# A neighbour-maximum kernel whose last late round stands behind its loop and makes no further one-hots

## The reference, cut to what matters

```
h = maximum(layernorm(x), 0)
for every node: the 25 first neighbours (lowest index j with adj[i, j] != 0)
agg = maximum over those neighbours of h[j]        # feature by feature
agg = maximum(agg, 0) where the node has 25 or fewer neighbours
out = x + relu(concat(h, agg) @ W + b)
```

## Time and profile before

| | us |
|---|---|
| three executions | 699.74, 697.43, 698.69 |
| their median | 698.69 |
| the profiled execution | 697.45 |
| its span in the profile | 695.7 |
| outside the span | 1.75 |

### The profile page before, as it was taken

How to read it: one execution, slowest core, us unless ns; L and a number is a source line. 1 busy time by engine, 2 the same in 40 slices (tenths; PEclk the granted TensorE clock), 3 DMA queues, 4 the chain that set the end, 5 groups by cost and what they waited for, 6 DMA issues and landing times.

```text
span 695.7 us, 10819 instructions
## 1 busy us (share of the span) xinstructions
PE 630.9 (91%) x3376; PEld 297.4 (43%) x3376; DVE 613.7 (88%) x813; ACT 472.3 (68%) x642; POOL 50.3 (7%) x41
## 2 busy tenths in 40 slices
PE   2479998999989999899999999899999999999976
PEld 2133443535445354443545344353535335353423
DVE  3368999899998999989998899989998899988997
ACT  2689478783777639775795947777497927959120
POOL 1300021000210002100030002100021000300000
PEclk9899999999999999999999999999999999999999
DMA  9520141510415103251303313151122411020100
GB/s 361 199 87 27 60 152 68 182 70 16 152 73 200 60 15 136 83 188 60 128 23 122 151 60 151 68 196 57 41 122 87 185 60 32 16 107 1 60 15 16
DMA packets 19127, 67.64 MB, mean 97 GB/s; under 512 B 4499, under 2 KB 7830, under 8 KB 16534
## 3 DMA queue, kind: packets, MB, share of 16 engines
q1 hardware_dynamic: 19094, 67.26, 25.7%
HBM read 42.08 MB, written 4.19 MB: 67 GB/s over the span
## 4 chain that ended last, share of the span: by engine, by line
PE 66%; DVE 16%; issue 10%; ACT 4%; DVEq 1%; DMA 1%; POOL 1%; ACTq 0%
PE picked L506 18%; PE picked L507 17%; PE ring L455 14%; DVE late_hot L684 4%; PE side L469 4%; PE ring L449 4%; DVE hot L659 4%; PE side L463 4%; DVE best L775 3%; DVE best L678 3%; PE final L534 2%; PE final L538 2%; PE final L491 1%; DMA adj_in<-in_adj_dram 1%; DVEq L771 1%
## 5 line engine op out<-in xcount | busy, mean ns | idle before, releaser
L678 DVE TENSOR_TENSOR best<-picked,best 128x1024 f32<-128x1024 f32 x224 | 270.5, 1218 | 38.2 <-PE picked L507 36.0
L506 PE MATMUL picked<-hot,h_hi 128*128 128x512 f16 x512 | 194.5, 380 | 15.0 <-DVE best L775 7.5
L507 PE MATMUL picked<-hot,h_lo 128*128 128x512 f16 x512 | 194.0, 379 | 0.0
L506 PE MATMUL picked<-late_hot,hi_skew 128*128 128x512 f16 x336 | 127.6, 380 | 13.1 <-DVE late_hot L684 8.2
L507 PE MATMUL picked<-late_hot,lo_skew 128*128 128x512 f16 x336 | 127.3, 379 | 0.0
L344 ACT ACTIVATE late_rank<-ring,late_bias 128x512 bf16<-128x512 f32 x128 | 81.4, 690 | 57.6 <-PE ring L455 57.6
L775 DVE TENSOR_TENSOR best<-picked,best 128x1024 f32<-128x1024 f32 x84 | 102.4, 1219 | 8.3 <-PE picked L507 8.2
L378 ACT COPY best<-picked 128x1024 f32<-128x1024 f32 x32 | 32.2, 1013 | 102.6 <-PE picked L507 102.6
L659 DVE TENSOR_SCALAR hot<-rank 128x4096 f16<-128x4096 bf16 x64 | 89.4, 1399 | 12.0 <-ACT rank L344 12.0
L349 ACT ACTIVATE past<-side,bias_cut 128x512 bf16<-128x512 f32 x128 | 88.3, 690 | 6.2 <-PE side L469 4.9
L344 ACT ACTIVATE rank<-ring,bias_big 128x512 bf16<-128x512 f32 x128 | 83.1, 692 | 5.2 <-PE ring L455 4.9
(11 more groups left out here) (76 smaller groups left out, 562.1 us busy)
## 6 DMA issues: line engine op xcount, KB each, us to landing
adj_in<-in_adj_dram SPq DMA_DIRECT2D x16, 2048.0 KB, 7.7
late_skew<-late SPq DMA_DIRECT2D x32, 192.0 KB, 2.3
x_in<-in_x_dram SPq DMA_DIRECT2D x8, 512.0 KB, 8.5
xres<-in_x_dram SPq DMA_DIRECT2D x16, 256.0 KB, 7.8
late_skew<-late SPq DMA_DIRECT2D x16, 256.0 KB, 2.4
late_skew<-late SPq DMA_DIRECT2D x32, 128.0 KB, 2.0
out_dram<-xres SPq DMA_DIRECT2D x16, 256.0 KB, 2.0
late_skew<-late SPq DMA_DIRECT2D x32, 64.0 KB, 1.9
```

The costliest lines, as they stand in the source:

```text
L506: nc.tensor.matmul(dst, hi[:, slot, k, :], onehot, start=start, stop=False)
L507: return nc.tensor.matmul(dst, lo[:, slot, k, :], onehot, start=False, stop=stop)
L678: nc.vector.tensor_tensor(best[:, half, s, :, :], picked[s][:, :, :], best[:, half, s, :, :], ALU.max).then_inc(picked_read, 1)
```

## The change

The last round of each group no longer stands in the loop. TensorE gets a function `late_round`, DVE a function `take_late`. Both loops run one round fewer than the count (the constant at L667 is lowered by 1), but at least one; behind each loop the last round is written out. There DVE takes the two maxima and makes no one-hots. A group whose count was 1 now runs two rounds; the second finds one-hots that mark nothing. The register `rounds_done` goes up by one more behind the loop, and the wait for the one-hots no longer adds the group's number, since there is now one call of `make_late_hot` per round and half.

```diff
--- before.py
+++ after.py
@@ -539,6 +539,18 @@
                                             start=False, stop=(q == Q - 1))
                 last.then_inc(final_written, 1)
 
+            def late_round(g, done, r, slot):
+
+                for s in range(2):
+                    pe.wait_ge(picked_read, (g + 1) * READ - 1 + s)
+                    pe.wait_ge(late_hot_made[s], done + r + 1)
+                    pe.wait_ge(late_read[s], done + r + 1)
+                    for j in range(2):
+                        for i in range(LINK):
+                            k = s * HALF + j * LINK + i
+                            last = pick(picked[s][:, j, :], hi_skew, lo_skew, k, late_hot[:, k, :], slot, i == 0, i == LINK - 1)
+                    last.then_inc(late_written[s], 1)
+
             rounds_done = pe.alloc_register("pe_rounds_done")
             pe.reg_mov(rounds_done, 0)
 
@@ -592,16 +604,11 @@
                 pe.wait_ge(rounds_known, g + 1)
                 n = pe.value_load(late_rounds[0:1, u % 2:u % 2 + 1], min_val=1, max_val=NEIGHBOURS)
                 with pe.Fori(0, n) as r:
-                    for s in range(2):
-                        pe.wait_ge(picked_read, (g + 1) * READ - 1 + s)
-                        pe.wait_ge(late_hot_made[s], done + (r + (g + 1)))
-                        pe.wait_ge(late_read[s], done + r + 1)
-                        for j in range(2):
-                            for i in range(LINK):
-                                k = s * HALF + j * LINK + i
-                                last = pick(picked[s][:, j, :], hi_skew, lo_skew, k, late_hot[:, k, :], slot, i == 0, i == LINK - 1)
-                        last.then_inc(late_written[s], 1)
+                    late_round(g, done, r, slot)
                 pe.reg_add(rounds_done, rounds_done, n)
+                done = pe.snap(rounds_done)
+                late_round(g, done, 0, slot)
+                pe.reg_add(rounds_done, rounds_done, 1)
 
                 if more:
                     done = pe.snap(rounds_done)
@@ -664,7 +671,7 @@
                 nc.vector.tensor_reduce(late_most[:, :], final[:, :], AX.X, ALU.max).then_inc(late_reduced, 1)
                 dve.wait_ge(late_reduced, (CHAINS + 1) * g + 1)
                 for c in range(CHAINS):
-                    nc.vector.tensor_scalar(late_other[:, c:c + 1], late_most[c * PART:c * PART + 1, :], LINK * P / 2, 1.0, ALU.add,
+                    nc.vector.tensor_scalar(late_other[:, c:c + 1], late_most[c * PART:c * PART + 1, :], LINK * P / 2 - 1, 1.0, ALU.add,
                                             ALU.max).then_inc(late_reduced, 1)
                 dve.wait_ge(late_reduced, (CHAINS + 1) * (g + 1))
                 nc.vector.tensor_reduce(late_rounds[0:1, s:s + 1], late_other[:, :], AX.X, ALU.max).then_inc(rounds_known, 1)
@@ -677,6 +684,12 @@
                 dve.wait_ge(picked_written, g * USES + use + 1)
                 nc.vector.tensor_tensor(best[:, half, s, :, :], picked[s][:, :, :], best[:, half, s, :, :],
                                         ALU.max).then_inc(picked_read, 1)
+
+            def take_late(s, i, done, r):
+
+                dve.wait_ge(late_written[i], done + r + 1)
+                nc.vector.tensor_tensor(best[:, s, i, :, :], picked[i][:, :, :], best[:, s, i, :, :],
+                                        ALU.max).then_inc(late_read[i], 1)
 
             def make_late_hot(i, which):
 
@@ -771,11 +784,13 @@
                 n = dve.value_load(late_rounds[0:1, s:s + 1], min_val=1, max_val=NEIGHBOURS)
                 with dve.Fori(0, n) as r:
                     for i in range(2):
-                        dve.wait_ge(late_written[i], done + r + 1)
-                        nc.vector.tensor_tensor(best[:, s, i, :, :], picked[i][:, :, :], best[:, s, i, :, :],
-                                                ALU.max).then_inc(late_read[i], 1)
+                        take_late(s, i, done, r)
                         make_late_hot(i, numbers[:, bass.ds(r + 2, 1)])
                 dve.reg_add(rounds_done, rounds_done, n)
+                done = dve.snap(rounds_done)
+                for i in range(2):
+                    take_late(s, i, done, 0)
+                dve.reg_add(rounds_done, rounds_done, 1)
                 done = dve.snap(rounds_done)
                 for i in range(2):
                     dve.wait_ge(late_read[i], done + 1)
```

## The result

The changed kernel takes 704.91 us (median of 6 executions, 703.62 to 707.86), the kernel before 698.56 us on the same chip (697.43 to 699.74). The ratio is 1.0089, 95% interval 1.0072 to 1.0106: slower by some 6.3 us. The profiled execution took 705.20 us with a span of 703.5 us, against 697.45 and 695.7 before.

The account below looks back on a forecast made before the run. TensorE was taken as busiest, the DVE close behind and the bound in the last two groups. Second round +3.47, one-hots -0.7 and -1.18, refetch +3.5 gave +5.1 us: 702.5, or 703.8 us as a median; range 700.2 to 705.6.

Parts of the forecast that it names:

- step 1: DVE's 16 last late rounds: 32 one-hots go, 19.8 us less work, counted as no time.
- step 2: One-hot 0 of the last round in 14 groups: removing it gains 0.05 us each, -0.7 us.
- step 3: Last two groups, where the DVE is the bound: 0.59 us gained in each, -1.18 us together.
- step 4: Second round for the group with one: costs 3.47 us, bounds 3.0 and 3.96.
- step 5: Register waits and sums outside the loop: cost nothing, at most 0.2 us or so per group.
- step 6: TensorE's longer program at the outer loop's two wraps: refetch of 1.75 us each, +3.5 us, bounds 0 and 2.4 each.
- One sign: DVE's idle time around use 5: expected to grow from 0.59 towards 1.2 us.
- The reason given for the refetch: TensorE's outer loop: about 150 more instructions bring one more packet in the first pass, so the loop's head is lost.
- A: Outer loop's wrap: TensorE keeps its loop's head, no refetch; +1.6 us, 700.3 us; chance 0.17.
- B: Late rounds: both one-hots on the path in every group; 691.6 us, or 695.1 with the refetch; chance 0.04.
- C: Heavier wrap: TensorE's sequencer no longer ahead, straight rounds 0.2 us each; +9.2 us, 707.9 us; chance 0.04.
- the likeliest case: Whole kernel, with the refetch as priced: 703.8 us, bounds 701.3 to 705.6; chance 0.75.

Follow-up runs that it names:

- experiment 10: Changed kernel with its last late round making two one-hots again, into a tile nobody reads: 706.27 us, ratio 1.0101.
- experiment 1: Changed kernel with TensorE doing every late round in its loop again, at least two; the DVE's part stays: 701.31 us, ratio 1.0049.
- experiment 8: Kernel before with the DVE's part of the change alone, one-round group staying at one round: 697.12 us, ratio 0.9968.
- experiment 2: Kernel before with the count of late rounds raised to at least two, nothing else: 703.37 us, ratio 1.0056.
- experiment 3: Kernel before with 16 empty instructions in TensorE's outer loop, in its fourth group: 701.49 us, ratio 1.0034.
- experiment 4: Kernel before with 16 empty TensorE instructions behind the outer loop, in the fourteenth group: 698.57 us, ratio 0.9992.
- experiment 5: Kernel before with 64 empty instructions in TensorE's outer loop, in its fourth group: 714.36 us, ratio 1.0212.
- experiment 7: Kernel before with 64 empty instructions at the very start of TensorE's program, loop body length unchanged: 703.6 us, ratio 1.0071.
- experiment 12: Changed kernel with the branch hint on TensorE's outer loop, measured again beside the unhinted changed kernel: 700.22 us, ratio 1.0014.
- experiment 6: Changed kernel with a prefetch hint for the branch back to the head of TensorE's outer loop: 700.28 us, ratio 1.0016.
- experiment 11: Changed kernel itself, unaltered, measured again beside its hinted form: 706.83 us, ratio 1.0100.

## Why the prediction was right

The forecast was 703.8 us, in a range of 700.2 to 705.6; measured 704.91. The sign, the cause and both large terms hold. That the sum comes so near is in part luck. In the profiles the last L538 comes 7.57 us later, where the steps say 5.1: the refetch is 0.85 more than I had, the start 1.38 and the last two groups 0.82 more, both with the clock fallen, and the rest 0.57 less. By its steps:

1. DVE work down by 19.8 us, no time: x86 and x86 as forecast. Busy time is 599.6 rather than 594, because the records overlap on both sides: the take at 163.49 ends at 164.72 and the next begins at 165.29, so a one-hot of 742 ns adds only 0.57 us of busy time. With that the step gives 14.7 us; measured are 14.1. It is no part of the sum.
2. One-hot 0 at 0.05 us a group: near in size (-1.20 us over 13 groups is 0.09 each), but by luck. About 0.05 lies behind the last late matmul, the rest is 0.03 a round inside the loop, and both stand in experiment 10 too, where the one-hots are made. The kernels that have this gain (the changed one in all its forms, experiments 1 and 8) share the shorter sum in TensorE's wait for the one-hots; the others (2 to 5 and 7) lack both. That this is the reason was not tested by itself.
3. The last two groups at 0.59 each: measured 0.46 and 0.51. The fold follows the last take by 1.33 us (166.53 to 167.85 above, and 686.13 to 687.46 in experiment 8) and not by 1.25. In group 15 the gain did come through whole, as chosen, and not only the 0.27 of the lower bound; in the changed kernel's profile the clock then fell to 0.59 in 682:686, which took it back. Where it stayed at 1.00 and the one-hots are gone (experiments 1, 8 and 12), the stretch to group 16 is 0.48 to 0.49 us shorter than before.
4. The second round, +3.47: measured +3.38 in the changed kernel and +3.48 in experiment 2.
5. Register waits at nothing: right in size. The small gaps ahead of late rounds sum to 0.42 us; their cause stays open.
6. The refetch, 1.75 each: the existence was right, in 6 of 6 wraps of the changed kernel and its version with the one-hots. The size was too small. In profiles the pieces are 2.10 to 2.73, over the chosen 1.75 and in three of six over the upper bound of 2.4; with the fall of the clock the two wraps are 6.43 (2.44, 1.70 and 2.29) in one profile, and 6.6 by medians, where I had 3.5. The branch record was 3.6 to 4.2 us where I had 3.1 to 3.6. The packet was not the error: it took 1.03 and 1.08 us, and I had 1.20. The time around it is longer, 2.6 and 2.7 us (3.2 and 3.3 in experiment 10), where ACT's rows gave me 1.9 to 2.2. The packet that follows (216.4 us) starts after the branch record has ended at 215.65 and is no part of the wait.

One sign was misplaced. The DVE's idle time at use 5 should have grown from 0.59 towards 1.2 us; it is 0.59 still. The DVE waits out what it gained one step earlier, for the projection's result: 0.62 us at 174.96 in the row above, where in the profile of before it is 0.16.

The reason given for the refetch was half right. One packet more is fetched in the first pass, while TensorE is still in the loop, as the prediction said. What I took it to mean, as the expectation of experiment 5 puts it, was that the body no longer fits with its head. Experiment 6 shows that it does fit, and experiment 7 that a body of the old length is refetched when it lies elsewhere. What matters is whether the place where TensorE fetches ahead lies inside the loop. The Trainium skill (Runtime: NRT & Kernel Launch, Instruction fetch mechanics) says that prefetch is purely sequential into a first-in first-out memory. The packets bear that out without a hint; with it the prefetch past the end of the loop is not made, which the page doesn't say. That this packet pushes the head out is my reading of experiments 6 and 7 and of the packets at all 28 wraps; no row shows directly what TensorE holds.

Of the rivals, A (no refetch, +1.6 us) is what the hinted kernel is: +1.4 us by the second batch's medians and +0.4 by the third's, ratios 1.0016 and 1.0014. B needed slack in picked1, and the 0.66 us of waiting shows there was none. C is partly there: the range's upper end of 705.6 is passed by the 706.83 of experiment 11, and for the reason of a heavier wrap, though not by a sequencer that had fallen behind, as C had it, but by the clock. The lower end of the likeliest case, 701.3, took 1.1 us for a refetch; no row gives that number, and step 6 has 0 as its bound.

Open stays why the packet ahead is fetched at one wrap and not at the other of the same execution, in experiments 1 and 3. The miss goes with that packet both times. What decides on it no run tested.

## What to carry to other kernels

Before writing out a loop's last pass, count what the outer loop gains in code on the busiest engine, and look in the packets of that engine's queue whether its loop fetches in its second pass; instructions ahead of the loop can bring that about too (experiment 7). If it does, try the branch hint first: here one argument gave back 6.6 of 7.1 us, side by side. And peel a loop only on the engine that gains: the DVE's half alone is 1.7 us faster than before, the change with TensorE's half is 6.3 us slower. An operation named by the chain of waits is worth only the distance to the wait that ends next.

## What the runs showed of the hardware

- With a hint TensorE ran the second and third pass of a body with 128 more matmuls and weight loads (4 groups of 16 and 16) out of what it holds; without it, it fetched 19 packets in 195:545.
- A missed wrap on TensorE is a branch record of 3.5 to 4.8 us (214 to 245 ns when held) with a packet of its code that starts 1.0 to 1.8 us behind the branch's start, and 2.05 to 3.52 us more from L538 to use 4.
- Near the edge misses are not reproducible: 12 executions of one program spread over 699.2 to 706.9 us.
- Behind a refetch the granted clock fell in some executions and not in others, and the length of the idle time did not decide: with 2.44 us more to use 4 it fell (experiment 11), with 2.73 in experiment 10 it stayed at 1.00. A fall at 48 to 52 us (0.60 to 0.76 against 1.00) goes with a first late matmul 1.38 to 1.73 us later than before's (0.07 to 0.62 where the clock stayed up); it stands in seven of the thirteen profiles behind the prediction, whichever kernel it was, and may be why the times of the kernel before lie in clusters, 697.3 to 697.7, 698.3 to 699.1 and 699.3 to 700.4 us.
- An empty instruction with a record of 13 ns takes TensorE's sequencer 0.075 us (experiment 5).
